# A router and expert stage on one core: TensorE's tile loop with two tiles per turn, and list two's scatter without its wait for TensorE

## The chip, the cores and the metric

The kernel runs on one core of a Trainium2 chip (trn2). The metric is the device time of one execution in microseconds. Three executions of the kernel before took 1392.18, 1391.59 and 1389.78 us, median 1391.59.

## The reference, cut to what matters

A decoder layer over 128 sequences of 64 tokens, width 128, so 8192 rows: self attention in blocks of 64, cross attention, and a mixture of 8 experts of which each token takes the best two, with a layer norm after each of the three. Only the last part is touched:

```python
logits = einsum('btd,ed->bte', x, Wr); probs = softmax(logits)
topk_vals, topk_idx = top_k(probs, 2)          # two of eight experts
router_weights = topk_vals / topk_vals.sum(-1, keepdims=True)
h = silu(einsum('btd,efd->btef', x, W1))       # 128 -> 512
y = einsum('btef,edf->bted', h, W2)            # 512 -> 128
out = einsum('bte,bted->btd', gate, y)         # then layernorm(x + out)
```

## The kernel before, in words

The two attention layers fill the first 750 us; the change leaves them alone. Then a router part computes logits on TensorE and, on VectorE (DVE), for every token the places `pos[0]` and `pos[1]` where its row goes in the lists of rows sorted by expert.

**Lists and tiles.** The 64 blocks of 128 tokens are cut into four lists (`CHUNKS`: blocks 0 to 15, 16 to 39, 40 to 55, 56 to 63). Each list is a DRAM buffer `xd[c]` of 24, 32, 24 and 16 tiles of 256 rows, one expert per tile; `NTILE` is 96, `NJ` is 24 groups of four tiles. A row holds a token's high and low fp16 halves, 512 bytes.

**GpSimd (POOL)** scatters: for each block two indirect DMAs (L414), 128 in all, in the segments `SEGS` of at most 16 blocks. Before the first segment of list two it waits for `f_h` to reach 10, that is until TensorE has done the first product of five tiles (L408, L409). When list one's results are all stored, it gathers them back in bursts of four indirect DMAs (L427), two bursts for each group of 512 tokens.

**SyncE (SP)** loads each tile with one transposing DMA (L272) into one of four slots `xt[k]` (the tensors `cth` and `ctl` of the attention, seen again), each slot with a semaphore `ld_t[k]`, and stores each tile's result (L276). Tile i+4 is loaded once the first product of tile i is done.

**TensorE (PE)** walks the tiles in `four` (L687), four tiles per turn of a hardware loop (L712), 23 turns and a last one written out. For tile i its own instruction stream, its sequencer, issues `up` of tile i+1 and `down` of tile i by turns, for the two halves c of the hidden width. `up` is 12 matmuls of 256 columns per tile, `down` 24 of 128 columns; all go through `three` (L452, L453, L454). Which weights are read depends on the tile's expert: an integer word from `tabw` holds five expert numbers as base-8 digits. `load_word` (L660) reads the word once per turn, `offset` cuts a digit out of it, and small register instructions ahead of the matmuls add the constants of each weight slice. `three` multiplies high by high, high by low, low by high.

**ScalarE (ACT)** reads each half-tile twice through SiLU (L833, L834), DVE takes the low part (L1100) and evicts `down`'s result (L1105). From turn 11 on (`FJ`) DVE also combines a group of tokens per turn of four tiles, POOL gathers the next, and ACT writes the normalized group (L827).

Of the kernel before, what the change touches and what calls it, by code (L numbers as in the profile page):

```python
# [7 lines left out]
ALU = mybir.AluOpType  # L8
# [5 lines left out]
P = 128  # L14
# [20 lines left out]
NJ = NTILE // 4  # L35
FJ = max(CB[c + 1] // 4 + 1 - CHUNKS[c][0] // GT for c in range(NC - 1))
TAIL = NJ - FJ
NX = 24 + P + NTILE + KS + 4
# [49 lines left out]
def program(nc, x, ctx_in, mask, wstack, biases, w12, wr, const, out):  # L88
    ctx = ExitStack()
    with ctx:  # L90
        def sb(name, shape, dt):
            return ctx.enter_context(nc.sbuf_tensor(name, shape, dt))

        def sem(name):
            return ctx.enter_context(nc.semaphore(name))
# [25 lines left out]
        cth = [sb(f"cth{i}", [P, GTOK], F16) for i in range(2)]  # L121
        ctl = [sb(f"ctl{i}", [P, GTOK], F16) for i in range(2)]
# [32 lines left out]
        tabw = sb("tabw", [P, NJ], I32)  # L155
# [19 lines left out]
        xt = [q[:].rearrange("p (c r) -> p c r", c=2) for q in cth + ctl]  # L175
# [22 lines left out]
        ld_t = [sem(f"ld_t{n}") for n in range(4)]  # L198
# [36 lines left out]
        def _(sp):  # L235
# [35 lines left out]
            def load(c, n, k):  # L271
                sp.dma_start_transpose(xt[k], xd_v[c][bass.ds(n, 1)].rearrange("o r c -> (o r) c")).then_inc(ld_t[k], 16)  # L272
# [14 lines left out]
            def four(c, j, ahead, finished):  # L287
                for k in range(4):
                    if ahead < NC:
                        wait_apart(sp, f_h, 2 * (4 * j + k) + 2, ld_w, 96)  # L290
                        load(ahead, k if ahead > c else 4 * j + k + 4 - CB[c], k)
                    store(c, 4 * j + k - CB[c], k)
                if finished:
                    put(j - FJ - 1)

            arrived(0)
            for k in range(4):
                load(0, k, k)
# [18 lines left out]
        def _(pool):  # L317
# [130 lines left out]
        def _(pe):  # L448
# [210 lines left out]
            def load_word(j):  # L659
                return pe.value_load(tabw[0:1, bass.ds(j, 1)], min_val=0, max_val=E ** 5 - 1)  # L660
# [26 lines left out]
            def four(j, word, last):  # L687
                base = offset(word, 0)
                for k in range(4):
                    i, follow = 4 * j + k, not (last and k == 3)  # L690
                    if follow:
                        ahead = offset(word, k + 1)
                        pe.wait_ge(ld_t[(k + 1) % 4], 16 * (j + 1 + (k + 1) // 4))
                    for c in range(2):
                        if follow:
                            up((k + 1) % 4, c, ahead)
                        if k == 2 and c == 0 and not last:
                            pe.reg_mov(experts, load_word(j + 1))
                        down(i, k, c, base)
                    base = ahead  # L700

            def carried():
                return pe.snap(experts, min_val=0, max_val=E ** 5 - 1)
# [5 lines left out]
            for c in range(2):  # L709
                up(0, c, offset(word, 0))  # L710
# [137 lines left out]
        def _(dve):  # L848
# [238 lines left out]
            ets = wst[0:1, 3900:3900 + NTILE + 4]  # L1087
            powers = cst[0:1, NX - 4:NX].unsqueeze(1).to_broadcast([1, NJ, 4])
            digits = wst[0:1, 3072:3072 + NTILE].rearrange("p (j k) -> p j k", k=4)
            low_digits = wst[0:1, 3200:3200 + NJ]  # L1090
            link(nc.vector.memset(ets[:, NTILE:], 0.0))
            link(nc.vector.tensor_scalar(ets[:, 0:NTILE], ets[:, 0:NTILE], float(E - 1), None, ALU.min))
            link(nc.vector.tensor_tensor(digits, ets[:, 0:NTILE].rearrange("p (j k) -> p j k", k=4), powers, ALU.mult))
            link(nc.vector.tensor_reduce(low_digits, digits, AX.X, ALU.add))
            nc.vector.scalar_tensor_tensor(out=tabw[0:1, :], in0=ets[:, 4:].rearrange("p (j k) -> p j k", k=4)[:, :, 0], scalar=float(E ** 4),
# [126 lines left out]
```

## Time and profile before

| | us |
|---|---|
| median of three runs | 1391.59 |
| the profiled execution | 1394.73 |
| its span, first to last instruction | 1392.9 |
| scatter issued by POOL | 802.3 to 842.8, and 861.05 to 982.1 |
| first tile's first matmul | 846.95 |
| tile 46's result evicted | 1122.3 |

TensorE's clock was granted at 0.851 of full speed in the mean over the span. Times in the rows below are microseconds from the span's start, durations beside an instruction form are nanoseconds. "PE" is TensorE's matmul, "PEld" its weight load, and "PEldq" what its sequencer does itself: register instructions, the load of a word, branches. A matmul's shown duration overlaps with the next one's, so work is read from start to start.

### The profile page before, as it was taken

How to read it: one execution, taken by the hardware profiler on the slowest of the kernel's cores; microseconds unless marked ns; L12 is line 12 of the kernel's file. 1: busy time of each engine (PE TensorE's matmuls, PEld its weight loads, DVE VectorE, ACT ScalarE, POOL GpSimd, SP SyncE). 2: the span in 40 equal slices, each digit the busy share in tenths (PEclk: the TensorE clock that was granted, in tenths of full speed). 3: DMA queues.
4: the chain of work that ended last, by engine and by line, in shares of the span. 5: the costliest groups of instructions: out<-in, count | busy, mean ns of one | idle time of the engine just before them, and what ended most of it. 6: DMA issues, size and time to landing. Idle time of an engine off the chain costs nothing.

```text
span 1392.9 us, 30650 instructions
## 1 busy us (share of the span) xinstructions
PE 972.9 (70%) x10082; PEld 818.1 (59%) x10083; DVE 856.7 (62%) x2598; ACT 728.6 (52%) x1364; POOL 444.5 (32%) x536
## 2 busy tenths in 40 slices
PE   4888888884999999999997205111497977677740
PEld 2777777773888878888885104000386866456530
DVE  3788888884788888888885712000254566566452
ACT  3766666663867767767664203000275755456531
POOL 3132333332010010100104273777102054554555
PEclk8998888896999999999995557555698999999985
DMA  6930000000000000000000013111133334444431
GB/s 192 289 82 15 15 15 15 15 8 20 11 11 19 9 19 9 9 19 9 0 2 1 1 47 77 55 57 51 45 93 79 90 93 100 101 105 98 98 87 53
DMA packets 157231, 73.69 MB, mean 53 GB/s; under 512 B 76034, under 2 KB 151042, under 8 KB 157188
## 3 DMA queue, kind: packets, MB, share of 16 engines
q1 hardware_dynamic: 148996, 56.34, 15.5%
q0 software_dynamic: 8192, 16.79, 4.3%
q8 instruction: 24, 0.39, 0.1%
q14 instruction: 19, 0.16, 0.0%
HBM read 22.76 MB, written 37.75 MB: 43 GB/s over the span
## 4 chain that ended last, share of the span: by engine, by line
PE 34%; DVE 19%; ACT 14%; another core or an unknown queue 13%; issue 12%; POOL 4%; DMA 1%; SPq 1%; DVEq 0%; ACTq 0%; POOLq 0%
PE bank L452 8%; PE bank L453 7%; PE bank L454 7%; PE bank L554 4%; DVE at L927 3%; DVE X L1004 3%; ACT XTa L748 3%; DVE mx L911 3%; ACT qzh L748 3%; PE bank L540 3%; POOL xd L414 2%; PE bank L531 2%; DVE st L994 2%; POOL wst L427 1%
## 5 line engine op out<-in xcount | busy, mean ns | idle before, releaser
L427 POOL DMA_INDIRECT wst<-yd,pos x128 | 129.3, 1011 | 218.4 <-DVE z L1119 112.6
L452 PE MATMUL bank<-XTa,qzh 128*128 128x128 f16 x768 | 146.1, 226 | 37.7 <-ACT XTa L748 37.7
L927 DVE TENSOR_TENSOR at<-bank,rc 64x32 f32<-64x32 f32 (+1 forms) x768 | 153.5, 200 | 14.4
L762 ACT ACTIVATE pr<-bank 128x512 f32<-128x512 f32 x192 | 114.0, 594 | 78.3 <-PE bank L531 77.1
L911 DVE TENSOR_REDUCE mx<-bank 128x8 bf16<-128x512 f32 x192 | 132.9, 692 | 29.0 <-PE bank L454 23.4
L833 ACT ACTIVATE pr<-bank 128x512 f32<-128x512 f32 x96 | 57.5, 599 | 178.0 <-remote 90.4
L414 POOL DMA_INDIRECT xd<-XTa,pos x128 | 123.1, 962 | 83.3 <-issue 65.1
L454 PE MATMUL bank<-XTa,qzl 128*128 128x128 f16 x768 | 146.8, 227 | 0.0
L453 PE MATMUL bank<-XTa,qzh 128*128 128x128 f16 x768 | 146.6, 226 | 0.0
L766 ACT ACTIVATE pt<-bank 128x512 f32<-128x512 f32 x192 | 113.2, 590 | 61.6 <-PE bank L540 61.2
L833 ACT ACTIVATE xs<-bank 128x512 f32<-128x512 f32 x96 | 57.4, 598 | 163.8 <-remote 101.1
L1100 DVE TENSOR_TENSOR xtl<-xs,xth 128x512 f16<-128x512 f32 x96 | 66.4, 694 | 120.3 <-ACT xth L834 113.9
L554 PE MATMUL bank<-vz_cross,pt 128*128 128x36 f32 x1024 | 126.5, 270 | 0.0
L540 PE MATMUL bank<-ident,pr 128*128 128x128 f32 x768 | 122.8, 284 | 4.8 <-ACT pr L762 4.7
L554 PEld LDWEIGHTS bank<-vz_cross,pt 128*128 128x128 f32 x1024 | 125.5, 193 | 0.0
L349 POOL CAST mbf<-mraw 128x512 bf16<-128x512 uint8 x16 | 9.8, 614 | 322.5 <-PE bank L454 322.5
L452 PEld LDWEIGHTS bank<-XTa,qzh 128*128 128x128 f16 x768 | 78.1, 102 | 55.2 <-issue 41.8
L452 PE MATMUL bank<-W,xth 128*128 x384 | 75.5, 227 | 47.1 <-DVE xtl L1100 27.9
L341 POOL TENSOR_SCALAR ve<-mv 128x4 f32<-128x4 f32 x48 | 12.8, 267 | 275.3 <-DVE mv L998 246.6
L540 PEld LDWEIGHTS bank<-ident,pr 128*128 128x128 f32 x768 | 90.3, 146 | 16.0 <-ACT pr L762 9.5
L452 PE MATMUL bank<-cth,W 128*128 128x256 f16 x192 | 55.0, 286 | 59.6 <-DMA cth<-xd 56.5
L531 PE MATMUL bank<-mx,negI 128*128 128x512 bf16 x192 | 75.7, 394 | 25.3 <-DVE mx L911 24.0
(203 smaller groups left out, 3091.8 us busy)
## 6 DMA issues: line engine op xcount, KB each, us to landing
yd<-at SPq DMA_DIRECT2D x96, 128.0 KB
xd<-blank SPq DMA_DIRECT2D x2, 3072.0 KB, 20.7
X<-x_dram SPq DMA_DIRECT2D x16, 256.0 KB, 2.8
wst<-w_dram SPq DMA_DIRECT2D x16, 256.0 KB, 2.7
xd<-blank SPq DMA_DIRECT2D x1, 4096.0 KB, 28.6
cin<-ctx_in_dram SPq DMA_DIRECT2D x16, 256.0 KB, 2.9
out_dram<-z SPq DMA_DIRECT2D x16, 256.0 KB
xd<-blank SPq DMA_DIRECT2D x1, 2048.0 KB, 21.4
```

The lines of the kernel that those rows point to most:

```text
L414: nc.gpsimd.indirect_dma_start(out=xd[chunk_of(t)], out_offset=bass.IndirectOffsetOnAxis(ap=pos[k][:, t:t + 1], axis=0), in_=xhl[:, t, :], ...
L427: nc.gpsimd.indirect_dma_start(out=yg[k][:, t, :], out_offset=None, in_=yd[chunk_of(n)], in_offset=bass.IndirectOffsetOnAxis(ap=pos[k][:, ...
L452: nc.tensor.matmul(out_, lh, rh, start=start, stop=False, **kw)
L453: nc.tensor.matmul(out_, lh, rl, start=False, stop=False, **kw)
L454: return nc.tensor.matmul(out_, ll, rh, start=False, stop=stop, **kw)
L540: m = nc.tensor.transpose(TB[u % 2][:, b * P:(b + 1) * P], pr[u % 2][:, b * P:(b + 1) * P], ident[:])
L554: m = nc.tensor.matmul(PVB[u % 2][:, b * W:(b + 1) * W], pt[u % 2][:, c], v, start=True, stop=True)
L762: nc.scalar.activation(pr[u % 2][:], SC[u % 2][:], ACT.Exp).then_inc(s["ex"], 1)
L766: nc.scalar.activation(pt[u % 2][:], TB[u % 2][:], ACT.Copy).then_inc(s["ph"], 1)
L833: nc.scalar.activation(s32[n % 4][:], bank[n % 4][:], ACT.Silu, scale=IWS)
L911: nc.vector.tensor_reduce(mx[u % 2][:], SC[u % 2][:].rearrange("p (r k) -> p r k", k=S), AX.X, ALU.max).then_inc(s["mx"], 1)
L927: m = nc.vector.tensor_tensor(dst, src, r, ALU.mult)
```

## The change

TensorE's function `four` becomes `two`: two tiles per turn, 47 turns and a last one written out. A word holds three expert numbers, is read every two tiles, and is read in the first tile of a turn, between `up` and `down` of its second half. As four slots do not fit into a loop of two tiles as constants, the slots become one tensor `ct`, and `up` computes the slot's column from the loop's counter. Two load semaphores take the place of four; for that SP waits, before each load, that the load two tiles earlier has landed. VectorE builds 48 words in place of 24. On POOL the wait for `f_h` at 10 is gone.

```diff
+NW = NTILE // 2
-        cth = [sb(f"cth{i}", [P, GTOK], F16) for i in range(2)]
-        ctl = [sb(f"ctl{i}", [P, GTOK], F16) for i in range(2)]
+        ct = sb("ct", [P, 4 * GTOK], F16)
+        cth = [ct[:, i * GTOK:(i + 1) * GTOK] for i in range(2)]
+        ctl = [ct[:, (2 + i) * GTOK:(3 + i) * GTOK] for i in range(2)]
-        ld_t = [sem(f"ld_t{n}") for n in range(4)]
+        ld_t = [sem(f"ld_t{n}") for n in range(2)]
...
             def load(c, n, k):
-                sp.dma_start_transpose(xt[k], ...).then_inc(ld_t[k], 16)
+                sp.dma_start_transpose(xt[k], ...).then_inc(ld_t[k % 2], 16)
+
+            def landed(n, k):
+                wait_apart(sp, ld_t[k % 2], n * 8 + 16 - 8 * (k % 2), ld_w, 96)
...
                         wait_apart(sp, f_h, 2 * (4 * j + k) + 2, ld_w, 96)
+                        landed(4 * j + k + 2, k)
                         load(ahead, k if ahead > c else 4 * j + k + 4 - CB[c], k)
...
             for k in range(4):
+                if k >= 2:
+                    sp.wait_ge(ld_t[k % 2], 16)
                 load(0, k, k)
...
             for n, (t0, t1) in enumerate(SEGS):
-                if t0 == CHUNKS[1][0]:
-                    pool.wait_ge(f_h, 10)
...
-            def up(k, c, base):
+            def up(k, c, base, slot):
                 n = 2 * (k % 2) + c
+                rows = [ct[:, bass.ds(slot * GTOK + h * RT, RT)] for h in range(2)]
                 for h in range(2):
                     w = base + (2 * c + h) * 2 * P
-                    m = three(H[n][:, h * RT:(h + 1) * RT], (W1[:, bass.ds(w, P)], W1[:, bass.ds(w + P, P)]),
-                              (xt[k][:, 0, :], xt[k][:, 1, :]), start=h == 0, skip_group_check=True)
+                    m = three(H[n][:, h * RT:(h + 1) * RT], (W1[:, bass.ds(w, P)], W1[:, bass.ds(w + P, P)]), rows, start=h == 0, skip_group_check=True)
...
-            def four(j, word, last):
+            def two(j, word, last):
                 base = offset(word, 0)
-                for k in range(4):
-                    i, follow = 4 * j + k, not (last and k == 3)
+                for k in range(2):
+                    i, follow = 2 * j + k, not (last and k == 1)
                     if follow:
                         ahead = offset(word, k + 1)
-                        pe.wait_ge(ld_t[(k + 1) % 4], 16 * (j + 1 + (k + 1) // 4))
+                        slot = 2 * ((j + k) % 2) + 1 - k
+                        pe.wait_ge(ld_t[1 - k], 16 * (j + 1 + k))
                     for c in range(2):
                         if follow:
-                            up((k + 1) % 4, c, ahead)
-                        if k == 2 and c == 0 and not last:
+                            up(k + 1, c, ahead, slot)
+                        if k == 0 and c == 1 and not last:
                             pe.reg_mov(experts, load_word(j + 1))
                         down(i, k, c, base)
...
-            with pe.Fori(0, NJ - 1) as j:
-                four(j, carried(), False)
-            four(NJ - 1, carried(), True)
+            with pe.Fori(0, NW - 1) as j:
+                two(j, carried(), False)
+            two(NW - 1, carried(), True)
```

The rest of the diff makes the words of three digits on VectorE with the same number of instructions on 48 elements in place of 24.

## Rows read from the trace of the kernel before

**Rows 1.** Busy time by stage: us, then each engine's busy time, granted clock, DMA.

```profile
core 0: us, PE busy (x) PEld busy (x) DVE busy (x) ACT busy (x) POOL busy (x), PEclk, DMA share, GB/s
865.00:996.00 131.00, 17.69 (x64) 6.53 (x63) 2.92 (x5) 3.26 (x6) 89.03 (x93) 0.51 0.13 50
1004.00:1050.00 46.00, 44.85 (x580) 39.84 (x577) 27.70 (x49) 34.70 (x65) 0.00 (x0) 1.00 0.35 92
1120.00:1340.00 220.00, 158.41 (x1748) 124.53 (x1745) 127.69 (x366) 119.05 (x244) 119.62 (x133) 0.95 0.41 99
```

**Rows 2.** Timeline of POOL, then its scatter line as a group.

```profile
841.85 0.96 POOL L414 DMA_INDIRECT xd<-XTa,pos  x1 [0.30 <-issue]
861.05 1.07 POOL L414 DMA_INDIRECT xd<-XTa,pos  x1 [18.25 <-PE bank L454]
...
981.15 0.95 POOL L414 DMA_INDIRECT xd<-XTa,pos  x1 [0.30 <-issue]
...
L414 POOL DMA_INDIRECT xd<-XTa,pos x128: 954/958/1388, 802.3 to 981.1; - x128
```

**Rows 3.** Timeline in the scatter: TensorE, then ScalarE's next half-tile.

```profile
865.48 0.27 PE L454 MATMUL bank<-ctl,W 128*128 128x256 f16 x1
...
917.04 0.60 ACT L833 ACTIVATE pr<-bank 128x512 f32<-128x512 f32 x1 [38.94 <-remote]
```

**Rows 4.** The word's load (L660) by TensorE's sequencer, stretch 923 to 925.

```profile
L660 PEldq FUSED_REGOPS  x2: 42/100/157, 923.3 to 923.8; - x2
L660 PEldq TENSOR_LOAD <-tabw x1: 313/313/313, 923.4 to 923.4; - x1
```

**Rows 5.** DMA queues: first 848 to 862, then 862 to 1300.

```profile
q8 instruction: 2, 0.03, 0.8%
...
q1 hardware_dynamic: 71400, 23.74, 20.9%
q0 software_dynamic: 5856, 12.00, 9.8%
q14 instruction: 4, 0.03, 0.0%
```

**Rows 6.** Timeline of TensorE in one undisturbed turn, and three turns on.

```profile
1018.72 0.27 PE L454 MATMUL bank<-ctl,W 128*128 128x256 f16 x1
1019.27 0.23 PE L452 MATMUL bank<-W,qh 128*128 x1 [0.28 <-issue]
...
1019.46 0.22 PE L454 MATMUL bank<-W,ql 128*128 x1
...
1019.97 0.22 PE L454 MATMUL bank<-W,ql 128*128 x1
1020.02 0.27 PE L452 MATMUL bank<-ctl,W 128*128 128x256 f16 x1
...
1020.57 0.27 PE L454 MATMUL bank<-ctl,W 128*128 128x256 f16 x1
...
1053.92 0.23 PE L452 MATMUL bank<-W,qh 128*128 x1 [0.19 <-issue]
```

**Rows 7.** TensorE's sequencer within one tile, 1014.95 to 1017.5.

```profile
L452 PEldq FUSED_REGOPS  x9: 46/46/142, 1015.0 to 1017.4; - x9
L453 PEldq FUSED_REGOPS  x4: 46/46/46, 1015.9 to 1017.3; - x4
L454 PEldq FUSED_REGOPS  x4: 46/46/46, 1015.2 to 1016.7; - x4
```

**Rows 8.** The sequencer at the next word, and the branch over all turns.

```profile
L660 PEldq FUSED_REGOPS  x2: 42/100/157, 1018.0 to 1018.6; - x2
L698 PEldq FUSED_REGOPS  x1: 50/50/50, 1019.0 to 1019.0; - x1
L712 PEldq COMPARE_BRANCH  x23: 79/218/232, 860.8 to 1330.0; - x23
```

**Rows 9.** Evictions: VectorE's timeline, then its line over 840 to 1125.

```profile
998.92 0.41 DVE L1105 COPY at<-bank 128x256 f32<-128x256 f32 x1
L1105 DVE COPY at<-bank x46: 414/417/425, 854.1 to 1122.3; 128x256 f32<-128x256 f32 x46
```

**Rows 10.** One write of a group per turn: ScalarE's timeline, the first and last of eleven.

```profile
1135.44 1.64 ACT L827 ACTIVATE z<-z,nmr,rstd 128x128 f32<-128x128 f32 x4
...
1318.11 1.65 ACT L827 ACTIVATE z<-z,nmr,rstd 128x128 f32<-128x128 f32 x4
```

**Rows 11.** One gather burst: POOL's timeline.

```profile
1138.86 1.15 POOL L427 DMA_INDIRECT wst<-yd,pos  x1 [5.38 <-DVE z L1119]
...
1142.81 0.94 POOL L427 DMA_INDIRECT wst<-yd,pos  x1 [0.30 <-issue]
```

**Rows 12.** The first tile load, from the chain of waits.

```profile
844.09 2.65 DMA cth<-xd
```

More of the change, by code:

```diff
@@ L35 @@
 NJ = NTILE // 4
+NW = NTILE // 2
 FJ = max(CB[c + 1] // 4 + 1 - CHUNKS[c][0] // GT for c in range(NC - 1))
 TAIL = NJ - FJ
-NX = 24 + P + NTILE + KS + 4
+NX = 24 + P + NTILE + KS + 2
 class Layer:
@@ L154, in program @@
         pos = [sb(f"pos{k}", [P, NT], U32) for k in range(2)]
-        tabw = sb("tabw", [P, NJ], I32)
+        tabw = sb("tabw", [P, NW], I32)
         mneg = sb("mneg", [P, GT], F32)
@@ L174, in program @@
         sl = [ql, kl] + xtl
-        xt = [q[:].rearrange("p (c r) -> p c r", c=2) for q in cth + ctl]
+        xt = [ct[:, k * GTOK:(k + 1) * GTOK].rearrange("p (c r) -> p c r", c=2) for k in range(4)]
         yb = [at[n // 2][:, 2 * (n % 2):2 * (n % 2) + 2, :] for n in range(4)]
@@ L271, in load @@
             def load(c, n, k):
-                sp.dma_start_transpose(xt[k], xd_v[c][bass.ds(n, 1)].rearrange("o r c -> (o r) c")).then_inc(ld_t[k], 16)
+                sp.dma_start_transpose(xt[k], xd_v[c][bass.ds(n, 1)].rearrange("o r c -> (o r) c")).then_inc(ld_t[k % 2], 16)
+            def landed(n, k):
+                wait_apart(sp, ld_t[k % 2], n * 8 + 16 - 8 * (k % 2), ld_w, 96)
             def store(c, n, k):
@@ L659, in load_word @@
             def load_word(j):
-                return pe.value_load(tabw[0:1, bass.ds(j, 1)], min_val=0, max_val=E ** 5 - 1)
+                return pe.value_load(tabw[0:1, bass.ds(j, 1)], min_val=0, max_val=E ** 3 - 1)
             def offset(word, k):
                 return pe.snap(word // E ** k % E * (2 * DFF))
-            def up(k, c, base):
+            def up(k, c, base, slot):
                 n = 2 * (k % 2) + c
+                rows = [ct[:, bass.ds(slot * GTOK + h * RT, RT)] for h in range(2)]
                 for h in range(2):
                     w = base + (2 * c + h) * 2 * P
-                    m = three(H[n][:, h * RT:(h + 1) * RT], (W1[:, bass.ds(w, P)], W1[:, bass.ds(w + P, P)]),
-                              (xt[k][:, 0, :], xt[k][:, 1, :]), start=h == 0, skip_group_check=True)
+                    m = three(H[n][:, h * RT:(h + 1) * RT], (W1[:, bass.ds(w, P)], W1[:, bass.ds(w + P, P)]), rows, start=h == 0, skip_group_check=True)
                 m.then_inc(f_h, 1)
@@ L702, in carried @@
             def carried():
-                return pe.snap(experts, min_val=0, max_val=E ** 5 - 1)
+                return pe.snap(experts, min_val=0, max_val=E ** 3 - 1)
             pe.wait_ge(r_tab, 1)
@@ L709, in _ @@
             for c in range(2):
-                up(0, c, offset(word, 0))
+                up(0, c, offset(word, 0), 0)
             pe.reg_mov(experts, word)
-            with pe.Fori(0, NJ - 1) as j:
-                four(j, carried(), False)
-            four(NJ - 1, carried(), True)
+            with pe.Fori(0, NW - 1) as j:
+                two(j, carried(), False)
+            two(NW - 1, carried(), True)
         @block.scalar
@@ L1086, in _ @@
                 link(nc.vector.tensor_reduce(et, past, AX.X, ALU.add))
[L1087 to L1090, printed above, removed]
+            ets = wst[0:1, 3900:3900 + NTILE + 2]
+            powers = cst[0:1, NX - 2:NX].unsqueeze(1).to_broadcast([1, NW, 2])
+            digits = wst[0:1, 3072:3072 + NTILE].rearrange("p (j k) -> p j k", k=2)
+            low_digits = wst[0:1, 3200:3200 + NW]
             link(nc.vector.memset(ets[:, NTILE:], 0.0))
             link(nc.vector.tensor_scalar(ets[:, 0:NTILE], ets[:, 0:NTILE], float(E - 1), None, ALU.min))
-            link(nc.vector.tensor_tensor(digits, ets[:, 0:NTILE].rearrange("p (j k) -> p j k", k=4), powers, ALU.mult))
+            link(nc.vector.tensor_tensor(digits, ets[:, 0:NTILE].rearrange("p (j k) -> p j k", k=2), powers, ALU.mult))
             link(nc.vector.tensor_reduce(low_digits, digits, AX.X, ALU.add))
-            nc.vector.scalar_tensor_tensor(out=tabw[0:1, :], in0=ets[:, 4:].rearrange("p (j k) -> p j k", k=4)[:, :, 0], scalar=float(E ** 4),
+            nc.vector.scalar_tensor_tensor(out=tabw[0:1, :], in0=ets[:, 2:].rearrange("p (j k) -> p j k", k=2)[:, :, 0], scalar=float(E ** 2),
                                            in1=low_digits, op0=ALU.mult, op1=ALU.add).then_inc(r_tab, 1)
@@ L1204 @@
     const[:, 2 * P + 24:2 * P + 24 + NTILE] = np.arange(NTILE)
-    const[:, 2 * P + 24 + NTILE:P + NX - 4] = np.arange(KS) * RT
-    const[:, P + NX - 4:] = E ** np.arange(4)
+    const[:, 2 * P + 24 + NTILE:P + NX - 2] = np.arange(KS) * RT
+    const[:, P + NX - 2:] = E ** np.arange(2)
     arrays = {
```

## The prediction
> **What bounds the kernel now.** I read the busy time by stage first. The expert stage (847 to 1340 us) has three parts [rows 1]. From 865 to 996 TensorE starts only 64 matmuls in 131 us; this is while POOL scatters lists two to four. From 1004 to 1050 POOL is idle and TensorE is busy nearly throughout. From 1120 to 1340 POOL gathers in bursts and TensorE is busy 158 of 220 us.
>
> In the first part (I call it the crawl) ScalarE shows what sort of stall it is. The half-tile whose last matmul is recorded at 865.48 reaches ScalarE only at 917.04 [rows 3]. By the program's order 31 matmuls and 31 weight loads are recorded in between, and the same count separates the two for the next half-tile. So matmuls enter a queue of some 62 entries and finish late; the sequencer fills that queue and then stands. It is not itself slow: when it comes to instructions that don't need the queue, at 923.3, the register instruction, the word's load (0.31) and the next register instruction follow within 0.5 us [rows 4]. The crawl begins 3 to 4 us after POOL's first indirect DMA at 861.05 and ends some 14 us after the last at 981.15 [rows 2]. Every gather burst later brings a short one.
>
> In the undisturbed part the bound is the sequencer. A word's stall repeats at 1019.27 and at 1053.92, three turns on, so a turn of four tiles takes 11.55 us, 2.89 per tile [rows 6]. The matmuls alone need less: nine starts of 128 columns in 0.51 us are 0.057 each, five of 256 columns in 0.55 are 0.11 [rows 6]; 24 and 12 of them make 2.66 per tile, 10.6 per turn. The sequencer needs 2.4 us from the first register instruction of one tile to that of the next [rows 7], about 2.42 at finer reading, and in it are 16 register instructions of `three` and three others (L675, L677), back to back: 2.42 / 19 = 0.12 us each, with the matmuls' dispatch inside it. The word costs from 1018.0 to 1019.0 less the 0.1 that stands there otherwise, some 0.87 [rows 8]. So 11.55 - 4 x 2.42 - 0.87 leaves 1.00 for the loop's turn: branch (0.22), counter and what comes late after it.
>
> **The change part by part.** I work against the profiled execution (1394.7 us, span 1392.9, so 1.8 around it); it lies 3.1 above the median of 1391.6, and I carry the difference over.
>
> *Two tiles per turn.* 24 more words and 24 more turns, each pair 0.87 + 1.00 = 1.87 us of the sequencer. Two tiles then need 2 x 2.42 + 1.87 = 6.71, 3.36 per tile against 2.66 of matmul work: nothing covers it outside the crawls. The Trainium skill ("Advanced Engine Details and Errata", Control Flow Timing) has a compare-and-branch at about 108 ns; the trace has 218 ns, and 1.00 us for the whole turn. By the page alone, 24 branches would be an estimated 2.6 us; the sum goes by the rows.
>
> *The slot as a computed column.* No row shows it. Now `up` has register instructions only for its two weight slices. In the change each `up` call has two more addresses, `rows[0]` and `rows[1]`. From below: nothing, if they are folded into the instructions there are. From above: two for each of the two h, 8 per tile. The nearest row is `down`, whose moving operand is W2 at two computed addresses; it spends two register instructions per h and uses them again for the second 128 rows [rows 7]. I take that: two per call, 4 per tile, 4 x 0.12 = 0.48. Per tile 3.36, 3.84 or 4.32 for none, 4 or 8.
>
> *The scatter without its wait.* POOL's 128 DMAs are 1.262 apart: 802.3 + 128 x 1.262 = 963.8 in place of 982.1, 18.2 earlier [rows 2]. But the six tiles whose `up` and `down` ran before the crawl now meet it from the first matmul on. The crawl lets some 64 matmuls pass, under two tiles. Before, the seventh tile was evicted at 998.92 [rows 9], 16.8 after POOL's last issue; now the third is, at 980.6. Four more tiles at the old 2.89 cost 11.6 of the 18.2 won: -6.7 by itself. Bounds: 0, if the crawl's tail grows with 128 DMAs over 96; -18 if TensorE gets as far as before.
>
> *SP.* One more wait per load, before it nothing but the next load and, behind that, the store of a tile. A load was issued two tiles (5.8 us) before the next one of its parity and the first took 2.65 [rows 12], so it has landed. Loads are four tiles ahead; the cover is gone only if a landing takes over 5.8. Its three or four extra register instructions lie within SP's idle time. I take 0, bounds 0 and +5. Loads 2 and 3 wait for loads 0 and 1, about 3 us, before tile 2 needs them. *VectorE's words:* same instructions, before POOL's data arrive: 0.
>
> **The sum.** Let s be the sequencer's time per tile. Undisturbed part: the 46th tile is evicted at 1122.3, 39 tiles and 123.4 us after the seventh [rows 9]. Now it is 43 tiles after the third: 980.6 + 123.4 + 39 (s - 2.89) + 4 s. For s = 3.84 that is 1156.4, +34.1.
>
> Gather part: ten turns from 1135.44 to 1318.11 are 18.27 each [rows 10], 6.7 over 11.55, so a burst loses 3.36. A burst lasts 4.9 [rows 11] and a crawl ends about 0.9 after it, 5.8; in this time the sequencer can still put 31 matmuls, 0.86 of a tile, into the queue, 2.5 us. 5.8 - 2.5 = 3.3 is just what is lost. So a turn is 4 s + 2 (5.8 - 0.86 s), and 12.5 turns grow by 12.5 x 2.28 (s - 2.89): +27.1 for s = 3.84.
>
> Together +61: 1391.6 + 61 = **1453 us**. With s = 3.36 it is 13.5 + 13.4 = +27, 1419; with 4.32 it is 54.8 + 40.8 = +96, 1487. If the queue hides the sequencer wholly in the gather part, the three are 1405, 1426 and 1446.
>
> **The rivals.** *(a) The shorter loop ends the crawl (faster).* The place is TensorE's code: 390 instructions per turn before, some 200 now; if the crawl is code coming in late, a loop that stays resident would run at full speed beside POOL. The price: tiles go on from 847, the 46th at about 847 + 46 x 3.84 = 1024 in place of 1122, and turns of 15.4 in place of 18.27 win another 36: 1391.6 - 98 - 36 = 1258, and 1220 with s = 3.36. It decides if code fetches fall into the crawls. Against it: between 862 and 1300 not one packet of the queue with 16 KB blocks (two at 848 to 862), only four of the other instruction queue [rows 5], yet every burst crawls, and the sequencer ran 923.3 to 924 at full speed [rows 4]. A rule of the Trainium skill would speak for it ("Runtime: NRT & Kernel Launch", Instruction fetch mechanics): a taken branch whose target is outside the resident pages forces a fetch before execution goes on. The trace shows no such fetch after 862.
>
> *(b) The loop's cost is light.* Addresses fold into existing instructions, or the queue hides more: 1400 to 1430.
>
> *(c) The scatter's gain decides (slightly faster).* If TensorE makes in the longer crawl as many tiles as before and the loop's price is covered by the matmuls, the wait's 18.2 come through, less a few: 1375 to 1388. It decides if s stays under some 2.95. Against: sequencer already over the matmuls, with no wait in it.
>
> *(d) The addresses are not shared:* 8 or more register instructions per tile, 1475 to 1500, more if each matmul gets its own.
>
> **How the numbers follow.** The forecast case (1430 to 1475) 0.44, (b) 0.24, (d) 0.13, (a) 0.08, (c) 0.08, no change 0.03. A range of 1385 to 1492 leaves out (a), most of (c) and the top of (d), about 0.18. A measurement of this kernel tells 0.2%, about 2.8 us, from no change. Faster 0.16, same 0.03, slower 0.81; the likeliest case's own range is 1430 to 1475.
>
> **What would show it.** Between 1000 and 1100 the distance from one word's load to the next over two tiles: 7.7 us (6.7 in (b), 8.6 in (d)). Register instructions at L453 within `up`, absent now. POOL's last scatter near 964, the third eviction near 981, ScalarE's groups 20.4 apart. Wrong if the matmuls from 850 to 960 follow each other at 0.06 to 0.11 us: then (a) holds. Wrong in size if the sequencer's register instructions are no longer 0.12 apart.

## The result, and the profile after

The changed kernel takes 1413.18 us in the median (1412.31 to 1416.09, four runs), beside 1390.82 of the kernel before: ratio 1.0164, 95% interval 1.0146 to 1.0182. On two chips of the later runs it was 1.0198 (1.0162 to 1.0234) and 1.0182 (1.0142 to 1.0223). So it is slower as forecast, but by 22 us and not by 61. The profiled execution took 1416.09 us, span 1414.3, which is 21.4 more than the profiled one of before.

Busy time by stage, the kernel after (columns as in [rows 1], whose stretches these answer):

```profile
860.00:980.00 120.00, 17.09 (x70) 7.23 (x70) 3.53 (x7) 5.23 (x10) 78.17 (x82) 0.50 0.12 47
1000.00:1050.00 50.00, 44.31 (x506) 34.18 (x504) 23.99 (x42) 30.39 (x56) 0.00 (x0) 1.00 0.28 73
1150.00:1360.00 210.00, 157.06 (x1656) 116.39 (x1656) 118.45 (x340) 112.89 (x232) 110.62 (x123) 0.96 0.39 99
```

The crawl (the part in which TensorE barely gets on while POOL scatters) is as slow as before: 70 matmuls in 120 us, where [rows 1] has 64 in 131. The undisturbed part is where the kernel changed: 506 matmuls in 50 us, where [rows 1] has 580 in 46. In the gather part they are 7.9 per us, 7.9 before.

POOL's scatter as a group, then VectorE's evictions as groups over three stretches (durations in ns, then the first and the last start):

```profile
L420 POOL DMA_INDIRECT xd<-XTa,pos x128: 954/958/1390, 801.1 to 961.9; - x128
...
L1112 DVE COPY at<-bank x3: 418/419/425, 934.7 to 980.6; 128x256 f32<-128x256 f32 x3
L1112 DVE COPY at<-bank x46: 415/418/425, 934.7 to 1140.6; 128x256 f32<-128x256 f32 x46
L1112 DVE COPY at<-bank x51: 415/417/426, 1140.6 to 1368.0; 128x256 f32<-128x256 f32 x51
```

From here the 21.4 us come apart. The 46th eviction stands at 1140.6, +18.3 to [rows 9]. From it to the 96th it is 227.4; the kernel before has 1345.8 there, 223.5 after its 46th: +3.9. Behind the last tile 0.8 comes back. Further traces of the two kernels have 219.2 before and 222.6 and 225.0 after for this second stretch, so traces of one kernel lie up to 4.8 us apart and the +3.9 is hardly more than that.

TensorE's sequencer over two tiles of the undisturbed part (1003 to 1010.15, 7.15 us: the three lines of `three`, then the loop), and its word loads from 1003 to 1041:

```profile
L458 PEldq FUSED_REGOPS  x18: 46/46/168, 1003.1 to 1009.9; - x18
L459 PEldq FUSED_REGOPS  x10: 46/46/57, 1003.5 to 1009.8; - x10
L460 PEldq FUSED_REGOPS  x8: 46/46/57, 1003.2 to 1010.1; - x8
L719 PEldq COMPARE_BRANCH  x1: 218/218/218, 1004.0 to 1004.0; - x1
...
L666 PEldq TENSOR_LOAD <-tabw x5: 306/327/341, 1007.0 to 1035.6; - x5
```

The five words are (1035.6 - 1007.0) / 4 = 7.15 us apart, 3.57 per tile. And `three` has (18 + 10 + 8) / 2 = 18 register instructions per tile, two more than the 16 of before. The forecast had four more.

Last, what TensorE waited for in the gather part, first the kernel before (1120 to 1340), then the one after (1140 to 1360): in total, times, longest.

```profile
PE bank L452 <- DVE xtl L1100: 24.9, 25, 1.4
PE bank L452 <- DVE ql L1100: 13.5, 10, 2.3
PE bank L452 <- issue: 13.4, 22, 1.5
PE bank L453 <- issue: 5.0, 9, 1.2
PE bank L454 <- issue: 4.2, 6, 1.3
```

```profile
PE bank L458 <- issue: 23.7, 50, 1.1
PE bank L458 <- DVE xtl L1107: 15.8, 23, 1.2
PE bank L458 <- DVE ql L1107: 6.4, 9, 1.3
PE bank L459 <- issue: 5.0, 7, 1.2
PE bank L460 <- issue: 3.8, 7, 1.2
```

TensorE in the kernel before waited 38.4 us of 220 for VectorE's low part, which I had not looked at. After, this wait is 22.2, and "issue" is 32.5 in place of 22.6: the longer loop fills time in which TensorE had stood waiting. "Issue" is idle time that no other engine ended. It holds the sequencer's own time and the crawl of the bursts together; under "What the crawl is worth in the gather part" below, a kernel with the same loop of four tiles has none of it on a chip without the crawl, so before the change it was the crawl's.

### The profile page after: what moved, and what is told of

The parts are those of the page before. It is cut to its first block, busy times and chain, and to the rows that moved or that the text cites. A ratio compares the mean times of both kernels' runs of the same rounds, so it can differ in the third digit from the quotient of the medians.

```text
span 1414.3 us, 31202 instructions
## 1 busy us (share of the span) xinstructions
PE 992.7 (70%) x10082; PEld 814.8 (58%) x10083; DVE 857.8 (61%) x2598; ACT 728.6 (52%) x1364; POOL 445.4 (31%) x536
## 4 chain that ended last, share of the span: by engine, by line
PE 37%; issue 21%; DVE 20%; ACT 13%; POOL 4%; another core or an unknown queue 1%; DMA 1%; DVEq 1%; SPq 1%; ACTq 0%; POOLq 0%
PE bank L458 9%; PE bank L460 8%; PE bank L459 8%; PE bank L560 4%; DVE at L934 3%; DVE X L1011 3%; ACT XTa L755 3%; DVE mx L918 3%; ACT qzh L755 3%; PE bank L546 2%; POOL xd L420 2%; PE bank L537 2%; DVE st L1001 2%; ACT xth L841 1%
## 5 line engine op out<-in xcount | busy, mean ns | idle before, releaser
L458 PE MATMUL bank<-ct,W 128*128 (+1 forms) x384 | 109.4, 285 | 89.4 <-DMA ct<-xd 57.1
L918 DVE TENSOR_REDUCE mx<-bank 128x8 bf16<-128x512 f32 x192 | 132.9, 692 | 27.8 <-PE bank L460 22.2
L459 PE MATMUL bank<-ct,W 128*128 (+1 forms) x384 | 109.4, 285 | 17.9 <-issue 17.8
L460 PE MATMUL bank<-ct,W 128*128 (+1 forms) x384 | 109.4, 285 | 15.1 <-issue 15.0
## 6 DMA issues: line engine op xcount, KB each, us to landing
xd<-blank SPq DMA_DIRECT2D x1, 2048.0 KB, 18.2
```

Source lines behind the costliest of these rows:

```text
L458: nc.tensor.matmul(out_, lh, rh, start=start, stop=False, **kw)
L459: nc.tensor.matmul(out_, lh, rl, start=False, stop=False, **kw)
L460: return nc.tensor.matmul(out_, ll, rh, start=False, stop=stop, **kw)
L918: nc.vector.tensor_reduce(mx[u % 2][:], SC[u % 2][:].rearrange("p (r k) -> p r k", k=S), AX.X, ALU.max).then_inc(s["mx"], 1)
```

## The experiments

A is the theory that in the gather part the sequencer's time is covered, B the forecast's, that it costs 2.28 us per turn and us of sequencer per tile. A1 and A2 are two forms of A: in A1 a turn there is TensorE's own matmuls plus what the bursts take, in A2 it is set by the work on the token groups (gather, combine, write), and TensorE follows. "Fifty tiles" is the time from the 46th to the 96th eviction.

**The parts one by one** (one chip; the kernel before 1387.86 us).

```diff
 # e1_wait_only, and e1_again on another chip: the kernel before
-                if t0 == CHUNKS[1][0]:
-                    pool.wait_ge(f_h, 10)
```

> The kernel before (four tiles per turn, words of five digits) without POOL's wait for f_h. Both theories: POOL's last scatter near 964 in place of 982, third eviction near 980.6, 46th near 1115.6 in place of 1122.3, turns in the gather part unchanged at 18.2. So -6.7 us on the median of before (about 1384). Bounds 0 (the crawl's tail grows) and -18 (TensorE gets as far as before). If instead the shorter loop had mattered for the crawl in the changed kernel, the matmuls let through by the crawl would differ here from the 70 of the changed kernel's stretch 860 to 980.

```diff
 # e2_two_with_wait: the kernel after
+                if t0 == CHUNKS[1][0]:
+                    pool.wait_ge(f_h, 10)
```

> The changed kernel with POOL's wait for f_h put back, so the two-tile loop, the short words, the computed slot and SP's landing waits alone. Seventh eviction again near 999, then 39 tiles at 3.57 (the 14.3 us per four tiles read from the changed kernel): 46th near 1145 to 1149. Theory A (in the gather part the queue in front of TensorE covers the sequencer wholly): the rest adds at most 4, total before +27, about 1418. Theory B (the gather part pays 2.28 us per turn for each us of s, as the prediction's formula has it, and the changed kernel won it back through an earlier scatter): the gather part adds 19, total before +43, about 1434.

```diff
 # e3_slot_only: the kernel before, four tiles per turn
-            def up(k, c, base):
+            def up(k, c, base, slot):
+                rows = [ct[:, bass.ds(slot * GTOK + h * RT, RT)] for h in range(2)]
...
+                        slot = 2 * ((j + j + (k + 1) // 2) % 2) + (k + 1) % 2
...
```

> The kernel before with one thing of the change: the four slots are one tensor and up computes the slot's column from the loop's counter; four tiles per turn, words of five digits, four load semaphores and POOL's wait as before. Two more register instructions per tile, 0.12 each: four tiles take 12.5 in place of 11.5 in the undisturbed part, +9 to +10 by the 46th eviction. Theory A: +10 in all, 1401. Theory B: another 12.5 x 2.28 x 0.24 = 7 in the gather part, +16, 1407.

```diff
 # e4_words_only: e2, four tiles per turn, so the slots are constants
-                        slot = 2 * ((j + k) % 2) + 1 - k
+                        slot = 2 * ((odd + k) % 2) + 1 - k
...
-            with pe.Fori(0, NW - 1) as j:
-                two(j, carried(), False)
+            with pe.Fori(0, NW // 2 - 1) as j:
+                two(2 * j, carried(), False, 0)
+                two(2 * j + 1, carried(), False, 1)
...
```

> The changed kernel with four tiles per turn, slots as constants and POOL's wait back: against before what is left is 24 more word loads on TensorE, two load semaphores with SP's landing waits, and 48 words built by VectorE. A word costs 0.87 of the sequencer, 0.22 per tile: four tiles take 12.4 in the undisturbed part, +8.5 by the 46th eviction. Theory A: +9 in all, 1400. Theory B: another 6, +15, 1406. If SP's landing waits cost anything, TensorE's first matmuls of a tile are released by SP's transposes and the turn is longer than 12.4.

| | ratio, 95% interval | four tiles undisturbed, us | scatter's start to 46th eviction | fifty tiles |
|---|---|---|---|---|
| before | 1 | 11.5 | 320.0 | 223.5 |
| e1 | 0.9944 (0.9915 to 0.9974) | 11.5 | 313.6 | 221.4 |
| e2 | 1.0160 (1.0110 to 1.0209) | 14.3 | 342.5 | 220.9 |
| e3 | 1.0052 (1.0025 to 1.0079) | 12.4 | 327.1 | 222.4 |
| e4 | 1.0036 (1.0008 to 1.0063) | 12.3 | 324.4 | 221.1 |

The wait is worth 6.4 us, where 6.7 was forecast. The slot adds 0.9 us per four tiles, the words 0.8, so the two more loop turns per eight tiles, one per four, have the remaining 14.3 - 11.5 - 0.9 - 0.8 = 1.1. Up to the 46th eviction e3 is 7.1 above the kernel before, where 9 to 10 was expected, and e4 4.4, where 8.5 was. The row of before is the first trace's, from another run than the four; b0_before, on yet another chip, has 318.8 and 219.2, so differences of 1 to 4 us in the two last columns tell little. In the fifty tiles all five lie within 2.6 us, though the sequencer's time differs by 2.8 us per four tiles; B wanted up to 20 us more for e2. The row of e1, its evictions from the 46th to the 96th as a group:

```profile
L1103 DVE COPY at<-bank x51: 415/418/425, 1114.3 to 1335.7; 128x256 f32<-128x256 f32 x51
```

e1_again, on a chip where the kernel before took 1386.88: 1379.13, ratio 0.9959 (0.9933 to 0.9985).

> The kernel before without the wait of POOL alone, on the chip of the run beside it. With the crawl: 0.994 as before. Without it: there is nothing to win on TensorE's side before the crawl, POOL is 18 us earlier; its gathers begin after list one's stores anyway, so 0.998 to 1.000.

**Shorter bursts** (the next three and the eight-tile loop on one chip; the kernel before 1387.47).

```diff
 # g1_half_gathers: the kernel before; g2_half_gathers_two: the kernel after
-                    for k in range(2):
+                    for k in range(1):
                         nc.gpsimd.indirect_dma_start(out=yg[k][:, t, :], ...)
-                dve.wait_ge(ld_y[u], 64 * (g + 1))
+                dve.wait_ge(ld_y[u], 32 * (g + 1))
```

> The kernel before with the gathers of the first expert alone: bursts of two indirect DMAs in place of four; the second expert's rows are not gathered and the combine reads what the buffer holds. Against the full gathers this takes about half of POOL's time in the gather part. Theory A1 (TensorE's own work there is matmuls at full rate plus what the bursts take, and the full queue covers the sequencer): 10.6 us of matmuls plus 2 x 1.9 in place of 2 x 3.8 makes 14.4 per turn of four tiles in place of 18.2, tiles 46 to 96 some 45 us faster. Theory A2 (the chain of a group of tokens, gather to combine to write, sets the turn and TensorE only follows): less than 2 us per turn. The scatter part is the same in both: scatter's start to the 46th eviction 320.

> The changed kernel with the gathers of the first expert alone, the second expert's rows left out, as in the run beside it. There the sequencer needs 14.3 us per four tiles (2 words, 2 turns). A1: the cover is short now, max(14.3, 14.4) plus what a burst takes when the queue is not full, 14.5 to 16 per four tiles, so 0.3 to 1.5 more than the run of the kernel before with the same gathers, 4 to 18 us over the fifty tiles. A2: equal per four tiles, less than 3 us over the fifty tiles. The forecast's model (theory B, 2.28 us per turn and us of sequencer time) had predicted the difference to be there with the full gathers too, where it was 3.8 us.

Measured: 1350.89 (0.9743, 0.9708 to 0.9777) on the kernel before and 1368.12 (0.9878, 0.9847 to 0.9909) on the one after. The fifty tiles, evictions as a group, g1 and then g2:

```profile
L1105 DVE COPY at<-bank x51: 416/418/425, 1108.7 to 1304.7; 128x256 f32<-128x256 f32 x51
```

```profile
L1112 DVE COPY at<-bank x51: 416/418/425, 1124.3 to 1319.7; 128x256 f32<-128x256 f32 x51
```

They are 196.0 and 195.4: 23 to 28 less than the traces of the kernel before, 27 to 32 less than those of the one after, and equal, although 14.3 us of sequencer per four tiles stand in a turn of 15.7. A1 expected 45 us less and g2 4 to 18 us over g1; A2 expected them equal, but under 2 us off a turn, and it was 2.5 (18.2 to 15.7). What TensorE waited for in g1's fifty tiles, 1108.7 to 1304.7:

```profile
PE bank L452 <- DVE ql L1100: 26.7, 12, 2.9
PE bank L452 <- DVE xtl L1100: 14.2, 10, 2.1
PE bank L452 <- issue: 1.1, 2, 0.5
PE bank L454 <- issue: 1.0, 2, 0.5
```

With bursts of two the "issue" time is all but gone (2.1 us; 22.6 in the kernel before), so such short bursts make no crawl that can be seen. The wait for VectorE's low part stays, 40.9 us. In g2 it is 17.3 us, and "issue", now the sequencer, 19.4. The longer sequencer time thus goes into the wait for VectorE, and no crawl is needed to cover it.

**More work for the sequencer.**

```diff
 # p2_pad12: the kernel before, in down
+                for _ in range(6):
+                    pe.reg_mov(pad, 0)
```

> The kernel before with twelve more register moves per tile in TensorE's stream, six ahead of each product with the second weight; nothing else changes. At 0.12 us each this is +1.44 us per tile, so a turn of four tiles undisturbed goes from 11.5 to 17.3 us (less if a plain move is cheaper than the 0.12 worked out for the address instructions: at 0.06 it is 14.4). Theory A (in the gather part a full queue covers the sequencer): a turn there grows from 18.2 to at most 18.2 to 19.5 us, tiles 46 to 96 by under 15 us. Theory B: it grows by 2.28 x 1.44 = 3.3 us per turn, 41 us over the fifty tiles. Scatter's start to the 46th eviction: 320 + 39 x 1.44 = 376 in both, less what the gather part's first turn has of it.

1389.17, ratio 1.0011 (0.9987 to 1.0035), four tiles 11.7: the trace has not one instruction of that line, so moves of a constant into a register that is never read tested nothing. The next one reads a word where it had been carried:

```diff
 # p3_fresh_words, p3_again
-                        down(i, k, c, base)
-                    base = ahead
+                        down(i, k, c, offset(load_word(j), k))
```

> The kernel before, in which TensorE reads the word anew ahead of every product with the second weight (two more loads of a word per tile, their digits cut out again). Twelve idle register moves per tile had left no trace, neither in the instructions nor in the time, so this pads the sequencer with work that is used. At about 0.87 us a word, undisturbed four tiles go from 11.5 to some 17 to 19 us. Theory A (a turn in the gather part is the longer of the sequencer's time and of 18.2, what matmuls and bursts take): 18.2 to 19 per turn there, tiles 46 to 96 at most 15 us slower than 223. Theory B (2.28 us per turn and us of sequencer per tile, the forecast's): 21.5 to 22.5 per turn, some 45 us slower over the fifty tiles. The 39 tiles up to the 46th grow by 39 x 1.4 to 1.9 = 55 to 74 us in both.

> The kernel before with the word read anew ahead of every product, once more: on a chip without the crawl four tiles took 17.9 us from the first to the last, bursts or not. On a chip that crawls, theory A has 18.2 to 19.5 per turn in the gather part (the longer of 17.9 and 18.2), ratio about 1.03 (45 us in the first half, under 15 in the second). Theory B has 21.5 to 22.5 per turn there, ratio 1.06 or more. On one without the crawl: 1.064 as before.

The first run fell on the chip told of below, where it gave 1.0641 (1.0596 to 1.0685). The second, on a chip like the others (the kernel before 1386.24): 1455.53, ratio 1.0496 (1.0457 to 1.0536). Beside it on this chip ran the kernels before (b0) and after (b1) unchanged. p3_again, its loop's branch in the undisturbed part and its fifty tiles; then the fifty tiles of b0 and of b1:

```profile
L711 PEldq COMPARE_BRANCH  x4: 218/218/218, 1008.5 to 1061.9; - x4
...
L1104 DVE COPY at<-bank x51: 416/418/425, 1180.6 to 1414.0; 128x256 f32<-128x256 f32 x51
```

```profile
L1105 DVE COPY at<-bank x51: 417/418/426, 1117.7 to 1336.9; 128x256 f32<-128x256 f32 x51
```

```profile
L1112 DVE COPY at<-bank x51: 410/418/425, 1140.7 to 1363.3; 128x256 f32<-128x256 f32 x51
```

So with 11.5, 14.3 and 17.8 us of sequencer per four tiles the fifty tiles take 219.2, 222.6 and 233.4. The first step costs 3.4 us where B has 20, the second 10.8 where B has 25, and 233.4 / 12.5 = 18.7 per turn is just over the sequencer's 17.8. That is A: next to nothing is paid until the sequencer's time comes near the turn.

**Fewer matmuls.**

```diff
 # m1_two_products, m1_again: in down, for three(...)
+                        nc.tensor.matmul(Y[...], sh[n][:, q], W2[:, bass.ds(w, P)], ...)
+                        m = nc.tensor.matmul(Y[...], sl[n][:, q], W2[:, bass.ds(w, P)], ...)
```

> The kernel before with two matmuls in place of three in the product with the second weight (high by low is left out): 8 matmuls of 128 columns fewer per tile, 0.45 us of matmul work per tile, 1.8 per four tiles. It asks what sets a turn of 18.2 us in the gather part, where the last runs gave 15.7 with half bursts whether the sequencer needs 11.5 or 14.3. Theory A1 (TensorE's own work, matmuls plus what a burst takes): 18.2 - 1.8 = 16.4 per turn, fifty tiles some 20 us faster. Theory A2 (gather, combine, write of a group set the turn): 18 or more as before, fifty tiles under 5 us faster. Undisturbed four tiles: 10 to 11.5, as the sequencer's register instructions are nearly all still there. The crawl: if it counts matmuls, a tile gets through it with 8 fewer.

> The kernel before with two matmuls in place of three in the product with the second weight, once more, as it fell on the chip without the crawl. On a chip that crawls: A1 (matmuls plus what bursts take) 16.4 per turn in the gather part and some 20 us fewer over tiles 46 to 96; A2 (gather, combine, write of a group) under 5 us fewer. Undisturbed four tiles 10.0, as seen. Before the 46th: 27 to 35 tiles at 1.5 per four less is 10 to 13 us, and more if the crawl counts matmuls.

The first fell on the chip told of below (0.9963, 0.9935 to 0.9991). The second: 1357.34 beside 1386.88, ratio 0.9806 (0.9770 to 0.9843); undisturbed four tiles 10.0; fifty tiles 212.5 beside 219.4 of e1_again on the same chip:

```profile
L1105 DVE COPY at<-bank x51: 411/418/426, 1094.1 to 1306.5; 128x256 f32<-128x256 f32 x51
```

TensorE's waits in just these fifty tiles, 1094 to 1306.5:

```profile
PE bank L682 <- DVE ql L1100: 35.6, 18, 4.7
PE bank L682 <- DVE xtl L1100: 15.8, 13, 2.1
PE bank L682 <- issue: 10.0, 7, 5.4
```

6.9 us less, where A1 has 20 and A2 under 5. The wait for VectorE has 51.4 us of 212.5 here (first two rows), 38.4 of 220 in the kernel before: most of the time that the matmuls left was given to it. But there was a second change. TensorE's granted clock fell. The fifty tiles of m1_again and then of e1_again (columns as in [rows 1]):

```profile
1094.10:1306.50 212.40, 142.97 (x1381) 113.17 (x1378) 130.77 (x378) 119.34 (x242) 125.86 (x139) 0.83 0.43 103
1108.50:1327.90 219.40, 159.25 (x1781) 125.89 (x1778) 130.70 (x378) 119.21 (x243) 122.11 (x138) 0.95 0.42 100
```

With 0.83 of full speed in place of 0.95 the matmuls that are left take longer (one of 256 columns at L454 314 ns in the mean over 1120 to 1340, 291 in the kernel before), and how much of A1's 20 us went there was not measured. So this run alone doesn't refute A1; g1 and g2, at 0.95 and above, speak against it more plainly.

**Eight tiles per turn, without the wait.**

```diff
 # v1_eight: e1, and
-            with pe.Fori(0, NJ - 1) as j:
-                four(j, carried(), False)
+            with pe.Fori(0, NJ // 2 - 1) as j:
+                four(2 * j, carried(), False)
+                four(2 * j + 1, carried(), False)
+            four(NJ - 2, carried(), False)
```

> The kernel before without POOL's wait for TensorE (as in the run with that alone, -6.5 us from scatter to the 46th eviction) and with eight tiles per turn of TensorE's loop in place of four: 12 loop turns fewer, words as before. By the 1.00 us of a loop turn worked out from the rows, undisturbed eight tiles take 22.1 in place of 23.1 us, some 4 to 5 us over the 39 tiles up to the 46th. If the gather part covers the sequencer nothing more comes: 1390.8 - 6.5 - 4.5 = about 1380. If loop turns cost there too: another 6, 1374. If longer code is fetched at every turn: slower than the run with the wait alone (1384).

1380.37, ratio 0.9955 (0.9935 to 0.9974): it beats both kernels, but not e1 by anything that can be told. Eight tiles take 22.6 us in place of 23.0, so a loop turn saved in this way is worth 0.4 us, not 1.0.

**The crawl.** The experiments used five chips in all. On four the kernel before took 1386 to 1388 us; on the one on which p3_fresh_words, m1_two_products and s1_plain_scatter ran it took 1245.47 (1237.66 to 1252.65, thirteen runs). For a stretch in which POOL scatters in both (870 to 960) these are b0_before on an ordinary chip and then p3_fresh_words on that one:

```profile
870.00:960.00 90.00, 11.95 (x42) 4.25 (x42) 2.27 (x4) 2.17 (x4) 68.38 (x72) 0.50 0.15 58
```

```profile
870.00:960.00 90.00, 64.15 (x724) 48.72 (x722) 34.61 (x61) 43.42 (x80) 69.78 (x67) 1.00 0.36 107
```

POOL does nearly the same in both, 68 and 70 us of work; TensorE starts 42 matmuls in the first and 724 in the second, with more to do for its sequencer. One and the same kernel shows it too: from 860 to 960 m1_two_products starts 901 on that chip, m1_again 41 on an ordinary one. So whether there is a crawl depends on the chip; what differs between the chips is not known.

> The kernel before, unchanged, for its trace beside the next three. On the chip of the last three runs it took 1245 us in the median, where all chips before gave 1387 to 1391: 142 us less. There two of its variants showed no crawl while POOL scattered (901 matmuls from 860 to 960 us with two products, where the kernel before had some 60). If this chip crawls: 1385 to 1395, 64 matmuls or so in 130 us. If it does not: about 1245, TensorE busy from 850 on, four tiles in 11.5 us during the scatter.

> The changed kernel once more. On a chip that crawls: ratio 1.014 to 1.019 to the kernel before, as first measured. On one that does not crawl nothing covers the sequencer: 3.57 in place of 2.89 us per tile over up to 96 tiles is at most 65 us, and no scatter's gain comes in, since nothing waited in the crawl: ratio 1.03 to 1.052 if theory A's cover was the crawl's full queue and the gather part without it is bound by the sequencer; about 1.02 if the gather part there has another bound (gather, combine, write), so that only the first 46 tiles pay 31 us.

> The changed kernel a third time, on another chip. With the crawl: ratio 1.016 to 1.020, as twice before. Without it: 1.02 if the gather part has a bound of its own, so that only the first 46 tiles pay (46 x 0.68 = 31 us less what little is hidden), up to 1.05 if all 96 pay.

b1 and b2 fell on ordinary chips, so what the change costs where nothing crawls was not measured. What in the scatter makes the crawl on ordinary chips:

```diff
 # s1_plain_scatter, s1_again: the kernel before, rows stored in token order, so tiles hold other rows
-                        nc.gpsimd.indirect_dma_start(out=xd[chunk_of(t)], out_offset=..., in_=xhl[:, t, :], in_offset=None).then_inc(sent[n], 16)
+                        r0 = ((t - CHUNKS[chunk_of(t)][0]) * 2 + k) * P
+                        nc.gpsimd.dma_start(xd[chunk_of(t)][r0:r0 + P, :], xhl[:, t, :]).then_inc(sent[n], 16)
```

> The kernel before with 128 plain DMAs issued by POOL, each storing 128 rows one behind the other, in place of the 128 indirect ones: the rows then stand in token order and not by expert, so the tiles hold other rows. Same bytes, same queue, same waits. If the crawl of TensorE comes from the indirect DMAs (POOL working out 128 addresses each, or writes at scattered places): no crawl, TensorE makes its tiles at 11.5 per four from 850 on, the 46th is evicted before 1010 in place of 1122. If it comes from any DMA that POOL issues or from their bytes: the crawl stays, one matmul per 1.9 us while they last.

> The kernel before with plain DMAs in POOL's queue in place of the indirect ones in the scatter, once more (rows in token order, so tiles hold other rows). It could not tell anything on a chip without the crawl. On one that crawls: if the indirect form makes the crawl, the tiles go on at 11.5 per four from 850 on and the 46th is evicted before 1010; if any DMA that POOL issues does, one matmul per 1.9 us while they last.

s1_again, on the chip of b0: 1233.75 in one run, where b0 took 1385.91. POOL's line as a group, and the stretch in which it works:

```profile
L415 POOL DMA_DIRECT2D xd<-XTa x128: 540/540/810, 797.4 to 883.5; - x128
```

```profile
860.00:890.00 30.00, 29.11 (x378) 25.91 (x376) 18.18 (x32) 22.58 (x42) 24.04 (x46) 1.00 0.67 195
```

128 plain DMAs of the same bytes through the same queue, closer together and with 195 GB/s moving, leave TensorE at full speed: 378 matmuls in 30 us. It is the indirect form that makes the crawl (whether POOL's work on the addresses or the scattered writes does, this doesn't tell). s1_plain_scatter on the other chip took 1208.97 and had the same in the scatter (1230 matmuls from 860 to 960).

**What the crawl is worth in the gather part.** Both runs still gather with indirect DMAs, one on a chip that crawls, one on the chip that doesn't. So they show one kernel's fifty tiles with the bursts' crawl and without it: evictions as a group and TensorE's waits, s1_again and then s1_plain_scatter.

```profile
L1105 DVE COPY at<-bank x51: 416/418/426, 964.0 to 1184.8; 128x256 f32<-128x256 f32 x51
PE bank L452 <- DVE xtl L1100: 18.4, 20, 1.5
PE bank L452 <- DVE ql L1100: 16.1, 11, 2.8
PE bank L452 <- issue: 15.8, 20, 2.1
PE bank L453 <- issue: 7.8, 10, 1.8
PE bank L454 <- issue: 2.6, 6, 1.1
```

```profile
L1105 DVE COPY at<-bank x51: 408/418/424, 960.5 to 1160.7; 128x256 f32<-128x256 f32 x51
PE bank L452 <- DVE ql L1100: 30.8, 12, 3.7
PE bank L452 <- DVE xtl L1100: 13.2, 9, 3.1
```

The crawl takes 220.8 - 200.2 = 20.6 us, 1.6 per turn. Without it "issue" is gone, and a turn still has 200.2 / 12.5 = 16.0 us, 4.5 over the 11.5 of the undisturbed part. In that remainder TensorE waits 44.0 us for VectorE's low part, and one such wait shows why it comes late (s1_plain_scatter):

```profile
1053.10 1.65 ACT L827 ACTIVATE z<-z,nmr,rstd 128x128 f32<-128x128 f32 x4 [1.24 <-DMA out_dram<-z]
1054.99 0.61 DVE L1119 SCALAR_TENSOR_TENSOR z<-wst,X 128x128 f32<-128x128 f32 x2 [2.00 <-ACT z L827]
1055.64 0.61 DVE L1119 SCALAR_TENSOR_TENSOR z<-wst,z 128x128 f32<-128x128 f32 x2
1056.17 0.68 DVE L1100 TENSOR_TENSOR ql<-pr,qh 128x512 f16<-128x512 f32 x1
1057.10 0.23 PE L452 MATMUL bank<-W,qh 128*128 x1 [2.38 <-DVE ql L1100]
```

ScalarE writes a group only when the last one is stored, VectorE combines the next only when ScalarE has written, and the low part that TensorE needs stands behind that combine in VectorE's order. No run took the group's work out of the tiles' way, so this chain is read from the trace and not tested. On the same chip p3_fresh_words, with 17.9 us of sequencer per four tiles, has 220.6 in its fifty tiles (1051.8 to 1272.4), 17.6 per turn: past 16.0 the sequencer's time sets the turn.

## Why the prediction was right in its sign and wrong in its size

- *The scatter without its wait:* right. POOL's last DMA at 961.9 (forecast 963.8), the third eviction at 980.56 (980.6), and by itself -6.4 us up to the 46th eviction (-6.7); its medians are 4.2 and 7.8 us under the kernel before on two chips.
- *Words and loop turns:* right. 0.87 and 1.00 us of the sequencer per two tiles were the terms; e4 and the remainder give 0.8 and 1.1. The 1.00 does not carry over to the other direction (0.4 in v1). The Trainium skill ("Advanced Engine Details and Errata", Control Flow Timing) has 108 ns for a compare-and-branch; this kernel's rows have 218 again, and the turn as a whole costs two to five times that.
- *The slot:* the first step that failed. Its bounds were 0 and 8 register instructions per tile, and I took 4, from the row of `down`. There are 2, as `up`'s second half and the second call use the registers again. s is 3.57, between the 3.36 and 3.84 worked out, and 2 x 2.42 + 0.87 + 1.00 + 4 x 0.12 = 7.19 for two tiles is what the terms give with that count, measured 7.15. The 0.12 per instruction held (2.42 / 19 is 0.127, e3 has 0.9 / 8 = 0.11). With s = 3.57 the forecast's own formula has the 46th eviction at 980.6 + 123.4 + 39 x 0.68 + 4 x 3.57 = 1144.8, +22.5, measured +18.3; the forecast was +34.1. The rest of 4 us lies where the first two bursts of gathers fall into the "undisturbed" tiles. Evictions 23 to 31, before and after:

```profile
L1105 DVE COPY at<-bank x9: 414/417/424, 1045.8 to 1078.9; 128x256 f32<-128x256 f32 x9
L1112 DVE COPY at<-bank x9: 416/418/424, 1052.2 to 1087.1; 128x256 f32<-128x256 f32 x9
```

  These eight tiles grow by 34.9 - 33.1 = 1.8 us, where 8 x 0.68 = 5.4 was counted: beside the bursts the longer sequencer time is covered here too, and as VectorE combines no group yet, by the crawl and not by a wait for VectorE.
- *The gather part:* the step that failed most: +27.1 forecast, +3.9 measured. I took the 6.7 us that a turn has over 11.55 for the crawl of its bursts alone, found that the queue of 62 leaves just 3.3 per burst, and read the match as proof. The crawl is worth 1.6 us of a turn (s1_again against s1_plain_scatter). The larger part is a wait of TensorE for VectorE's low part, and a longer sequencer time fills it: with half bursts, where nothing crawls, the kernels before and after take 196.0 and 195.4. ScalarE's writes of a group, forecast 20.4 apart, are (1339.00 - 1154.08) / 10 = 18.49 apart. The variant "wholly hidden" stood in the sum, at 1405, 1426 and 1446, though it named the queue as the cover; with 2 instructions in place of 4 it lies at 1391.6 + 22.5 = 1414. That this is so near the measured 1413.18 is partly luck, as the +22.5 is 4 too high and the +3.9 is left out.
- *SP and VectorE's words:* nothing seen of them, e4 has both and costs what its words do.
- *The rivals:* (a) is wrong, the crawl lets 69 matmuls pass with four tiles per turn (e1, 860 to 980) and 70 with two, and it stops with another form of DMA at the same code. (b) is what happened in its number and half of its reasons: fewer register instructions than I took, and more cover, but by the wait for VectorE and not by the queue. (c) fell, as s is not under 2.95. (d) fell by the count.

The forecast case had 0.44 and (b) 0.24. The cover could have been had from the trace: the wait groups of one stretch show what fills the gaps. A term that rests on a numerical match should have been given its other end, nothing, as the likely one. The count of two register instructions stood in no row.

## What to carry to other kernels

Before charging an engine's added issue time to a stretch, list what that engine waits for in it: where it stands waiting for another engine's result, added time is free until it fills the wait. Here going from 11.5 to 14.3 us per turn of 18 cost 3.4 us in fifty tiles, and from there to 17.8 it cost 10.8 of the 44 added. A model of a stall that fits one number has not been tested by it; look at the same gaps by what ended them. And count computed addresses per value that the code reuses, not per call.

## What the runs showed of the hardware

While POOL scatters with indirect DMAs, TensorE gets through 33 to 42 matmuls in 90 us (b1 and b0, 870 to 960) on ordinary chips, four of the five of the experiments, and does not slow down on the fifth (724 in the same stretch, p3_fresh_words), where the whole kernel before is 142 us faster. Plain DMAs from the same queue do not do it, and neither can it be seen in gather bursts of two (g1: 2.1 us of "issue" in fifty tiles). The Trainium skill ("SBUF — State Buffer", two separate sides) says that within the engines only VectorE and GpSimd share a port, and that TensorE never waits on anyone; the crawl is a wait of TensorE beside work of GpSimd, so either it arises outside the SBUF or the rule lacks a case; no run here tells which. One register instruction of TensorE's sequencer takes 0.12 us from start to start, though it is shown with 0.046, and a loop turn 1.0 to 1.1 us with its branch of 0.218 when a turn of two tiles is added, 0.4 us when the turn of four is doubled (v1_eight).
